# Attention on one core: a head's turned probabilities handed over by PSUM bank, three pieces of keys each

## The chip, the cores and the metric

The kernel runs on one core of one Trainium2 chip. The metric is the device time of one execution in microseconds (us): the median of several runs.

## The reference

A stack of two layers over 8 sequences of 100 tokens, width 512. Each layer is a gated cross-attention to a context of 722 rows and then a gated mixture of experts. The first attention is masked by padding, the second is not. What bears on the change is the attention, 16 heads of width 32:

```python
q = _split_heads(query @ w_q.T + b_q)
k = _split_heads(key_in @ w_k.T + b_k)
v = _split_heads(value @ w_v.T + b_v)
scores = jnp.einsum('bhqd,bhkd->bhqk', q, k) / jnp.sqrt(jnp.float32(D_K))
scores = jnp.where(mask == 0, jnp.float32(-1000000000.0), scores)
attn = jax.nn.softmax(scores, axis=-1)
out = jnp.einsum('bhqk,bhkd->bhqd', attn, v)
```

Here b is 8, h is 16, q is 100 and k is 722.

## The kernel before

The function `attention` is called once a layer. Its last block handles the 8 batches one after the other (`over_batches`), with every order written out by hand, engine by engine, and semaphores between them. Heads are taken in 4 groups of 4 (`NG`, `HPC`). Keys are cut in two ways: for scores and softmax into two segments of 362 and 360 (`SEG`), for the transposes and the weighted values into six pieces of 128, the last one of 82 (`KC`).

A batch is a run of "halves" h: one segment of one group of heads. In each half TensorE does these things in this order (`body`): the scores of the half (L427); in even halves the weighted values of an earlier group (`weighted_values`, L458); a piece of the next batch's keys or values (`make_piece`, L321 and L325); the transposes of one head of the half two before (`transposed`, L439), called the first or even head here; a second piece; and the transposes of the second or odd head. The halves 4 to 11 make one turn of the loop. The last of them has no pieces, and has the output projection (L468) between its two heads. In the last batch of a layer there is no next batch, so pieces are left out everywhere.

VectorE takes maxima of the scores (L537 masked, L541 unmasked), then factors and the normalising of the probabilities (L571), and the second part of each piece (L343, L349). ScalarE does the exponentials (L661), the first part of each key piece (L334), the heads' outputs (L652), parts of the next context (L353), and the copies of turned probabilities out of PSUM (`turned`, L647). In its order for a half come first the copy of the odd head of the half before, then two exponentials, a small operation, two exponentials, and at the end the copy of the even head.

The turned probabilities of one head are six pieces of 100 columns. They lie in the tile `pt`, 128 partitions by 2 banks of PSUM, three pieces in each bank. There is one such tile:

```python
pt = cx.enter_context(nc.psum_tensor(env.name("pt"), [P, 2, 512], F32))
```

TensorE writes all six pieces and counts up `t_mm` once. ScalarE copies both banks into `pTs` by one instruction and counts up `t_out` once. The transposes of the next head wait for that, and `weighted_values` waits for all four heads of its group. The exponentials wait on `t_mm`, since they overwrite `probs` of a head that has been turned.

Of the kernel before, what the change touches and what calls it, by code (L numbers as in the profile page):

```python
# [10 lines left out]
ACT = mybir.ActivationFunctionType  # L11
# [3 lines left out]
P = 128  # L15
B, S, D = 8, 100, 512
SK = 722
H, DH = 16, 32
DC = D // P
HPC = P // DH  # L20
# [3 lines left out]
KC = -(-SK // P)  # L24
# [94 lines left out]
def attention(nc, env, layer, masked, w_q, b_q, w_k, b_k, w_v, b_v, w_o, b_o):  # L119

    with ExitStack() as cx:
        def sb(n, s, dt=F32):
            return cx.enter_context(nc.sbuf_tensor(env.name(n), s, dt))

        def sem(n):
            return env.semaphore(n)

        x, xnT, ident = env.x, env.xnT, env.ident
# [103 lines left out]
        probs = [sb(f"probs{n}", [S, SK]) for n in range(2 * HPC)]  # L232
        pTs = sb("pTs", [P, 2, HPC, KC, S])
# [7 lines left out]
        pt = cx.enter_context(nc.psum_tensor(env.name("pt"), [P, 2, 512], F32))  # L241
# [13 lines left out]
        t_mm, t_out, pv_mm, ao_ready = sem("t_mm"), sem("t_out"), sem("pv_mm"), sem("ao_ready")  # L255
# [20 lines left out]
        def keys_of(kc):  # L276
            return P if kc < KC - 1 else KTAIL

        def at_half(b, p, h):

            return (b, p, h // 2, h % 2) if h < NHALF else (b + 1, 1 - p, h // 2 - NG, h % 2)
# [4 lines left out]
        def bank_of_heads(g):  # L286
            return (pp, po)[g % 2]
# [63 lines left out]
        def split_high(act, part):  # L351
            k0, k1 = SPLIT[part]
            act.activation(ctx[0][:, :, k0:k1], raw[:, :, k0:k1], ACT.Copy).then_inc(high_ready, 1)  # L353
# [7 lines left out]
        def over_batches(body):  # L361

            for b in range(B):
                body(b, b % 2, min(2, B - 1 - b))

        with nc.Block() as block:
# [49 lines left out]
            def _(pe):  # L416
# [14 lines left out]
                def transposed(b, g, j, very_first=False):  # L431
                    pe.wait_ge(norm_done, b * (2 * H) + (g * HPC + j) * 2 + 2)
                    if very_first:
                        pe.wait_ge(pt_clear, 1)
                    else:
                        pe.wait_ge(t_out, b * H + g * HPC + j)
                    for kc in range(KC):
                        n = keys_of(kc)
                        last = pe.transpose(pt[0:n, kc // 3, (kc % 3) * S:(kc % 3 + 1) * S],  # L439
                                            probs[g % 2 * HPC + j][:, kc * P:kc * P + n], ident[0:S, 0:S])  # L440
                    last.then_inc(t_mm, 1)

                def weighted_values(b, p, g, more):
                    pe.wait_ge(t_out, b * H + HPC * (g + 1))
                    pe.wait_ge(piece_out, b * NPIECE + NPIECE)
                    if g == 0:
                        pe.wait_ge(res_done, b + 1)
                    elif more:
                        read_out = {1: ("k", 1, 0), 2: ("v", 0), 3: ("v", 2)}[g]
                        pe.wait_ge(piece_out, b * NPIECE + (NPIECE + PIECES.index(read_out) + 1))  # L450
                    elif g >= 2:
                        pe.wait_ge(ao_ready, b * NG + (g - 1))
                    bank = bank_of_heads(g)
                    for kc in range(KC):
                        n = keys_of(kc)
                        for j in range(HPC):
                            h = g * HPC + j
                            last = pe.matmul(bank[j * DH:(j + 1) * DH, 0:S], v[p][0:n, kc, h * DH:(h + 1) * DH],  # L458
                                             pTs[0:n, g % 2, j, kc, :], start=kc == 0, stop=kc == KC - 1,
                                             skip_group_check=True)  # L460
                    last.then_inc(pv_mm, 1)
# [179 lines left out]
            @block.scalar  # L641
            def _(act):

                def turned(b, g, j):
                    act.wait_ge(pv_mm, b * NG + g + 1)
                    act.wait_ge(t_mm, b * H + g * HPC + j + 1)
                    act.activation(pTs[:, g % 2, j, :, :].rearrange("k (a c) q -> k a (c q)", a=2),  # L647
                                   pt[:, :, 0:3 * S], ACT.Copy).then_inc(t_out, 1)

                def heads_out(b, g):  # L650
                    act.wait_ge(pv_mm, b * NG + g + 3)
                    act.activation(aoT[:, g, :], bank_of_heads(g)[:, 0:S], ACT.Identity, bias=bv[:, g:g + 1])\  # L652
                        .then_inc(ao_ready, 1)

                def exponents(b, g, seg, heads, first=False):
                    k0, k1 = SEG[seg]
                    for j in heads:
                        if not first:
                            act.wait_ge(t_mm, b * H + (g * HPC + j - 7))
                        act.wait_ge(max_ready, b * (2 * H) + ((g * 2 + seg) * HPC + j + 1))  # L660
                        act.activation(probs[g % 2 * HPC + j][:, k0:k1], ps[j][0:S, 0:k1 - k0], ACT.Exp,  # L661
                                       bias=less_max[:, g, seg, j:j + 1], scale=-1.0 if masked else 1.0,
                                       accum_out=sums[:, g, seg, j:j + 1]).then_inc(exp_done, 1)

                def shares(b, g):
                    act.wait_ge(apart_done, b * NG + g + 1)
                    act.activation(share[:, g, :, :], apart[:, g, :, :], ACT.Exp).then_inc(share_done, 1)

                def next_high(b, part):
                    act.wait_ge(ctx_in, b * 16)  # L670
                    act.wait_ge(piece_mm, b * NPIECE + (PIECES.index(LAST_READER[part]) + 1 - NPIECE))
                    split_high(act, part)

                def first_piece(*what):
                    piece_high(act, what, 0)
                first_piece("k", 0, 0)
                first_piece("k", 0, 1)
                exponents(0, 0, 0, range(HPC), True)
                first_piece("k", 1, 0)
                first_piece("k", 1, 1)  # L680
                exponents(0, 0, 1, range(HPC), True)
                shares(0, 0)
                first_piece("k", 2, 0)
                first_piece("k", 2, 1)
                exponents(0, 1, 0, range(HPC), True)
                turned(0, 0, 0)
                turned(0, 0, 1)
                first_piece("k", 3, 0)
                exponents(0, 1, 1, range(HPC), True)
                shares(0, 1)  # L690
                first_piece("k", 3, 1)
                next_high(1, 0)
                turned(0, 0, 2)
                next_high(1, 1)
                next_high(1, 2)

                def body(b, p, left):
                    for h in HALVES:
                        bb, bp, g, seg = at_half(b, p, h)
                        tb, _, tg, late = at_half(b, p, h - 2)  # L700
                        lb, _, lg, l_late = at_half(b, p, h - 3)
                        pieces = BESIDE[h] if left else ()
                        if h < NHALF + 3 or left:
                            turned(lb, lg, 2 * l_late + 1)
                        active = h < NHALF or left
                        if active:
                            exponents(bb, g, seg, (0, 1))
                        if h % 2 == 0:
                            heads_out(b, h // 2 - 2)
                        elif pieces:  # L710
                            piece_high(act, pieces[0], b + 1)
                        if active:
                            exponents(bb, g, seg, (2, 3))
                            if seg == 1:
                                shares(bb, g)
                        if pieces and h % 2 == 0:
                            piece_high(act, pieces[0], b + 1)
                        if h < NHALF + 2 or left:
                            turned(tb, tg, 2 * late)
                        for what in pieces[1:]:  # L720
                            piece_high(act, what, b + 1)
                        if left == 2:
                            for part in {10: (0, 1), 11: (2,)}.get(h, ()):
                                next_high(b + 2, part)
                over_batches(body)
# [1164 lines left out]
```

## Time and profile before

| | us |
|---|---|
| median of 3 runs | 2391.73 |
| lowest and highest | 2384.24, 2392.93 |
| the profiled execution's own time | 2411.99 |
| its span | 2410.2 |
| TensorE busy (matmul) | 2152.3 |
| VectorE, ScalarE busy | 1293.2, 1007.2 |
| copies L647, 256 of them, busy | 172.5 |
| transposes L439, 1536 of them, busy | 182.7 |

The profile is of one execution. PE is TensorE's matmuls and PEld its weight loads, which run ahead of them. DVE is VectorE, ACT is ScalarE. In a row of the timeline the first number is the start in us, the second how long it took, the last (x6) how many alike instructions were merged; in brackets stands how long the engine was idle before, and what ended it. "Issue" is said where no semaphore event explains the end, and it can hide a wait that was over by the time of the next matmul.

### The profile page before, as it was taken

The numbers are of one execution on the slowest core, as the hardware profiler recorded it, in microseconds if no ns is written. First come the engines' busy times: TensorE is split into PE (matmuls) and PEld (weight loads), VectorE is DVE, ScalarE is ACT, GpSimd is POOL, SyncE is SP. The second block draws the span as 40 slices with busy tenths as digits, with TensorE's granted clock in tenths as the row PEclk, the third lists the DMA queues.
The fourth block names the chain that finished last, engine by engine and source line by source line (L and its number), as shares of the span: only waits on it lengthen the run. The fifth ranks groups of instructions, "written<-read, shape, count | busy, mean of one in ns | idle before, by whom it ended". The sixth has DMA issues, their size and how long they took to land. (4 is left out here: it accounts for less than half of the span.)

```text
span 2410.2 us, 39542 instructions
## 1 busy us (share of the span) xinstructions
PE 2152.3 (89%) x13422; PEld 1509.6 (63%) x13423; DVE 1293.2 (54%) x2824; ACT 1007.2 (42%) x2099; POOL 563.1 (23%) x556
## 2 busy tenths in 40 slices
PE   5999999977955999999939999999879988999995
PEld 3777777766922444444427777777669436777773
DVE  4677777765513222222256677777651106777776
ACT  2466666653200111111123666666533006566663
POOL 3000000002472455454521000000013202323321
PEclk9999999986987999999969999999969998999997
DMA  7000000003002999999641000000030006766642
GB/s 261 33 31 31 31 31 31 6 1 137 1 1 108 321 305 338 313 339 290 173 161 46 28 28 26 26 26 2 1 137 20 17 34 258 274 209 238 219 178 67
DMA packets 64819, 287.92 MB, mean 119 GB/s; under 512 B 11741, under 2 KB 12143, under 8 KB 45355
## 3 DMA queue, kind: packets, MB, share of 16 engines
q1 hardware_dynamic: 42842, 246.40, 27.2%
q0 software_dynamic: 21840, 39.69, 7.7%
q8 instruction: 87, 1.43, 0.2%
q14 instruction: 50, 0.40, 0.1%
HBM read 257.85 MB, written 33.96 MB: 121 GB/s over the span
## 5 line engine op out<-in xcount | busy, mean ns | idle before, releaser
L661 ACT ACTIVATE probs<-ps,less_max 100x362 f32<-100x362 f32 (+1 forms) x512 | 282.3, 563 | 145.2 <-DVE less_max L537 79.7
L1297 PE MATMUL pgu<-ring,xT 128*128 x560 | 267.4, 600 | 7.9 <-issue 4.3
L647 ACT ACTIVATE pTs<-pt 128x600 f32<-128x600 f32 x256 | 172.5, 674 | 160.4 <-PE pt L439 158.1
L439 PE MATMUL pt<-ident,probs 100*128 100x100 f32 (+1 forms) x1536 | 182.7, 256 | 43.9 <-ACT pTs L647 41.9
L439 PEld LDWEIGHTS pt<-ident,probs 100*128 100x128 f32 (+1 forms) x1536 | 153.2, 141 | 87.0 <-issue 59.5
L571 DVE TENSOR_SCALAR probs<-probs,factor 100x362 f32<-100x362 f32 (+1 forms) x512 | 178.1, 411 | 1.7
L1297 PEld LDWEIGHTS pgu<-ring,xT 128*128 128x128 f32 x560 | 99.7, 191 | 116.7 <-issue 116.5
L1343 ACT ACTIVATE sg<-pgu 128x256 f32<-128x256 f32 x70 | 26.8, 383 | 320.0 <-PE pgu L1297 320.0
L1654 DVE TENSOR_TENSOR ws_low<-w,ws_high 128x2048 fp32r<-128x2048 f32 x63 | 142.9, 2290 | 24.2 <-ACT ws_high L1585 24.2
L942 PE MATMUL pg<-wd,hT 128*100 128x512 f32 x256 | 115.1, 611 | 41.0 <-issue 37.1
L537 DVE CUSTOM_DVE_ANT_0 ps<-ps,madd 100x362 f32<-100x362 f32 (+1 forms) x256 | 128.7, 564 | 24.5 <-PE ps L427 24.3
L1373 DVE COPY hT<-ph 128x256 f32<-128x256 f32 x70 | 29.7, 424 | 197.6 <-PE ph L1303 197.6
L1311 PE MATMUL pd<-ring,hT 128*128 x280 | 132.9, 597 | 2.7 <-issue 1.8
L1585 ACT ACTIVATE ws_high<-w 128x2048 fp32r<-128x2048 f32 x63 | 120.6, 1918 | 24.8 <-PE pu L1534 20.6
L1249 POOL DMA_INDIRECT moe_sum<-y,sum_at x70 | 112.8, 1611 | 76.2 <-POOL sum_at L1244 51.5
L541 DVE TENSOR_REDUCE less_max<-ps 100x1 f32<-100x362 f32 (+1 forms) x256 | 118.4, 524 | 14.6 <-PE ps L427 13.5
L1365 DVE COPY xT<-px 128x512 f32<-128x512 f32 x71 | 49.1, 691 | 138.7 <-PE px L1279 138.7
L942 PEld LDWEIGHTS pg<-wd,hT 128*100 128x100 f32 x256 | 43.6, 172 | 111.4 <-issue 105.4
L1534 PE MATMUL pu<-ws_high,xT_high 128*128 128x512 f32 x240 | 108.2, 451 | 4.8 <-DVE ws_low L1654 4.8
L1339 ACT ACTIVATE y<-pd,slot_weight 128x512 f32<-128x512 f32 x70 | 48.1, 687 | 145.5 <-PE pd L1311 118.5
L1560 PE MATMUL pd<-w,hT 128*128 128x512 f32 x240 | 107.9, 592 | 0.0
L1477 POOL COPY index_now<-slot_token 128x1 uint32 (+1 forms) x16 | 31.2, 1947 | 318.6 <-PE px L1521 221.5
(261 smaller groups left out, 5070.2 us busy)
## 6 DMA issues: line engine op xcount, KB each, us to landing
ring<-in_l_ew SPq DMA_DIRECT2D x64, 1536.0 KB
w<-in_l_ew SPq DMA_DIRECT2D x64, 1024.0 KB, 8.2
xnT<-in_ctxT SPq DMA_DIRECT2D x14, 1444.0 KB, 6.6
wu<-in_l_up SPq DMA_DIRECT2D x2, 4096.0 KB, 12.7
b<-in_l_eb SPq DMA_DIRECT2D x8, 1024.0 KB, 4.6
moe_sum<-zrow SPq DMA_DIRECT2D x3, 2048.0 KB, 15.4
moe<-moe_sum SPq DMA_DIRECT2D x24, 200.0 KB
wd<-in_l_down SPq DMA_DIRECT2D x2, 2048.0 KB
```

The costliest lines, as they stand in the source:

```text
L439: last = pe.transpose(pt[0:n, kc // 3, (kc % 3) * S:(kc % 3 + 1) * S], probs[g % 2 * HPC + j][:, kc * P:kc * P + n], ident[0:S, 0:S])
L537: dve.tensor_tensor_reduce(out=scores, in0=scores, in1=madd[p][:, k0:k1], scale=-1.0, scalar=3.0e38, op0=ALU.add, op1=ALU.min, accum_out=l ...
L541: dve.tensor_reduce(least_of, scores, AX.X, ALU.max, negate=True).then_inc(max_ready, 1)
L571: dve.tensor_scalar(at, at, factor[:, g, seg, j:j + 1], None, ALU.mult).then_inc(norm_done, 1)
L647: act.activation(pTs[:, g % 2, j, :, :].rearrange("k (a c) q -> k a (c q)", a=2), pt[:, :, 0:3 * S], ACT.Copy).then_inc(t_out, 1)
L661: act.activation(probs[g % 2 * HPC + j][:, k0:k1], ps[j][0:S, 0:k1 - k0], ACT.Exp, bias=less_max[:, g, seg, j:j + 1], scale=-1.0 if masked ...
L942: last = pe.matmul(pg[n % 2][0:S, :], hT[:, hf * 8 + f, t * S:(t + 1) * S], wd[hf][:, f, :], start=f == 0, stop=f == 7)
L1249: pool.indirect_dma_start(out=env.moe_sum[p][:, :], in_=y[p][:, :], in_offset=None, compute_op=ALU.add, out_offset=bass.IndirectOffsetOnAx ...
L1297: last = pe.matmul(pgu[p][:, :], xT[p][:, c, :], wgu[c], start=c == 0, stop=c == DC - 1)
L1311: last = pe.matmul(pd[p][:, :], hT[p][:, f, :], wdn[f], start=f == 0, stop=f == FI - 1)
L1585: act.activation(ws[WS[q]][0][:, :, :], w[q][:, :, :], ACT.Copy).then_inc(w_high[q], 1)
L1654: dve.tensor_tensor(ws[WS[q]][1][:, :, :], w[q][:, :, :], ws[WS[q]][0][:, :, :].bitcast(F32), ALU.subtract).then_inc(w_low[q], 1)
```

## The change

The transposes of a head are handed over in two parts, one for each bank of `pt`. TensorE waits for the bank, writes three pieces, counts up `t_mm`, and does the same for the other bank. ScalarE copies each bank by an instruction of its own, 300 elements a partition in place of 600, and counts up `t_out` after each. All other waits on the two semaphores count twice as far, and so wait for the same as before.

```diff
-                    else:
-                        pe.wait_ge(t_out, b * H + g * HPC + j)
-                    for kc in range(KC):
-                        n = keys_of(kc)
-                        last = pe.transpose(pt[0:n, kc // 3, (kc % 3) * S:(kc % 3 + 1) * S],
-                                            probs[g % 2 * HPC + j][:, kc * P:kc * P + n], ident[0:S, 0:S])
-                    last.then_inc(t_mm, 1)
+                    for half in range(2):
+                        if not very_first:
+
+                            pe.wait_ge(t_out, 2 * (b * H + g * HPC + j) - 1 + half)
+                        for kc in range(3 * half, 3 * half + 3):
+                            n = keys_of(kc)
+                            last = pe.transpose(pt[0:n, half, (kc % 3) * S:(kc % 3 + 1) * S],
+                                                probs[g % 2 * HPC + j][:, kc * P:kc * P + n], ident[0:S, 0:S])
+                        last.then_inc(t_mm, 1)
...
-                    pe.wait_ge(t_out, b * H + HPC * (g + 1))
+                    pe.wait_ge(t_out, 2 * (b * H + HPC * (g + 1)))
...
-                    act.wait_ge(t_mm, b * H + g * HPC + j + 1)
-                    act.activation(pTs[:, g % 2, j, :, :].rearrange("k (a c) q -> k a (c q)", a=2),
-                                   pt[:, :, 0:3 * S], ACT.Copy).then_inc(t_out, 1)
+                    for half in range(2):
+                        act.wait_ge(t_mm, 2 * (b * H + g * HPC + j) + half + 1)
+                        act.activation(pTs[:, g % 2, j, 3 * half:3 * half + 3, :].rearrange("k c q -> k (c q)"),
+                                       pt[:, half, 0:3 * S], ACT.Copy).then_inc(t_out, 1)
...
-                            act.wait_ge(t_mm, b * H + (g * HPC + j - 7))
+                            act.wait_ge(t_mm, 2 * (b * H + (g * HPC + j - 7)))
```

## Rows read from the trace of the kernel before

**Rows 1.** Page, part 1: busy time, share of the span, instructions.
```profile
PE 2152.3 (89%) x13422; PEld 1509.6 (63%) x13423; DVE 1293.2 (54%) x2824; ACT 1007.2 (42%) x2099; POOL 563.1 (23%) x556
```

**Rows 2.** Windows, an inner and the last batch: length, busy by engine, granted clock, DMA.
```profile
334.00:391.00 57.00, 55.06 (x553) 44.85 (x552) 42.02 (x137) 36.78 (x99) 4.24 (x3) 1.00 0.10 33
506.00:563.00 57.00, 35.41 (x363) 23.30 (x361) 27.97 (x94) 23.63 (x63) 0.00 (x0) 0.72 0.08 26
```

**Rows 3.** Single lines' instructions: ns, lowest, median, highest; first and last start.
```profile
L97 ACT ACTIVATE xnT<-ln_pT x32: 503/504/506, 22.2 to 1784.0; 128x400 f32<-128x400 f32 x32
...
L647 ACT ACTIVATE pTs<-pt x256: 652/672/702, 80.0 to 1762.1; 128x600 f32<-128x600 f32 x128
...
L652 ACT ACTIVATE aoT<-pp,bv x32: 335/342/343, 105.9 to 1755.5; 128x100 f32<-128x100 f32 x32
...
L439 PE MATMUL pt<-ident,probs x1536: 247/249/429, 79.1 to 1761.7; 100*128 100x100 f32 x192
```

**Rows 4.** Timeline, ScalarE, a copy and the instruction behind it.
```profile
328.00 0.67 ACT L647 ACTIVATE pTs<-pt 128x600 f32<-128x600 f32 x1 [1.56 <-PE pt L439]
328.57 2.00 ACT L353 ACTIVATE ctx_high<-xnT 128x1024 fp32r<-128x1024 f32 x2
```

**Rows 5.** Timeline, ScalarE, unmasked layer: first exponential of an odd half.
```profile
1445.21 0.56 ACT L661 ACTIVATE probs<-ps,less_max 100x360 f32<-100x360 f32 x1 [0.57 <-DVE less_max L541]
```

**Rows 6.** Timeline, TensorE's weight loads: behind a key piece, and behind weighted values.
```profile
106.91 0.63 PEld L439 LDWEIGHTS pt<-ident,probs 100*128 100x128 f32 x6
...
324.33 0.19 PEld L325 LDWEIGHTS pp<-wv_high,ctx_high 128*128 128x128 f32 x1 [0.15 <-issue]
```

**Rows 7.** Timeline: the first head's copy and the second head's weight loads.
```profile
343.97 0.69 ACT L647 ACTIVATE pTs<-pt 128x600 f32<-128x600 f32 x1
...
344.78 0.52 PEld L439 LDWEIGHTS pt<-ident,probs 100*128 100x128 f32 x6 [0.23 <-issue]
...
350.86 0.52 PEld L439 LDWEIGHTS pt<-ident,probs 100*128 100x128 f32 x6 [0.27 <-issue]
...
1443.13 0.52 PEld L439 LDWEIGHTS pt<-ident,probs 100*128 100x128 f32 x6 [0.17 <-issue]
```

**Rows 8.** Timeline: weighted values behind scores, then a half without them.
```profile
365.70 0.68 PE L439 MATMUL pt<-ident,probs 100*128 100x100 f32 x6
366.31 0.42 PE L427 MATMUL ps<-kT_high,qb_high 32*100 32x362 f32 x4
366.48 0.67 ACT L647 ACTIVATE pTs<-pt 128x600 f32<-128x600 f32 x1 [2.65 <-PE pt L439]
367.20 1.02 PEld L458 LDWEIGHTS pp<-pTs,v 128*32 128x32 f32 x48 [0.47 <-ACT pTs L647]
...
373.59 0.41 PE L427 MATMUL ps<-kT_high,qb_high 32*100 32x360 f32 x4
...
374.27 0.19 PEld L325 LDWEIGHTS po<-wv_high,ctx_high 128*128 128x128 f32 x1 [0.26 <-issue]
```

**Rows 9.** Timeline at the turn of a batch.
```profile
336.54 0.68 ACT L647 ACTIVATE pTs<-pt 128x600 f32<-128x600 f32 x1
337.33 0.52 PEld L439 LDWEIGHTS pt<-ident,probs 100*128 100x128 f32 x6 [1.93 <-issue]
...
340.45 0.54 DVE L537 CUSTOM_DVE_ANT_0 ps<-ps,madd 100x362 f32<-100x362 f32 x1
```

**Rows 10.** Timeline in the last batches of both layers.
```profile
536.34 0.92 PEld L439 LDWEIGHTS pt<-ident,probs 100*128 100x128 f32 x6 [3.10 <-issue]
...
542.76 1.23 PE L439 MATMUL pt<-ident,probs 100*128 100x100 f32 x6 [0.91 <-ACT pTs L647]
544.09 0.67 ACT L647 ACTIVATE pTs<-pt 128x600 f32<-128x600 f32 x1 [1.48 <-PE pt L439]
544.87 0.92 PEld L439 LDWEIGHTS pt<-ident,probs 100*128 100x128 f32 x6 [1.23 <-issue]
...
1759.16 0.53 PEld L439 LDWEIGHTS pt<-ident,probs 100*128 100x128 f32 x6 [1.09 <-issue]
```

## The prediction

> **What bounds the kernel now.** I read the page first: TensorE is busy for 2152.3 of 2410.2 us [rows 1]. Whole-program shares say little of one stage, so the windows came next. In an inner batch of the masked attention (334 to 391 us) TensorE has work for 55.06 of 57.00 us at full clock, VectorE for 42.02 and ScalarE for 36.78; in the last batch of that layer, which has no next batch's keys and values to fill the gaps, TensorE is busy 35.41 of 57.00 us at a granted clock of 0.72 [rows 2]. So inner batches are bound by TensorE except for small pauses, and the last one by the chain from engine to engine. Then the timeline was walked through one batch, looking for idle time ahead of TensorE's weight loads (the PEld rows), and for who ended each. A turned head passes TensorE, PSUM, ScalarE's copy, and TensorE again, and pauses of four kinds hang on it.
>
> **Prices of the pieces.** The change replaces one copy of 600 elements by two of 300: 256 ScalarE instructions more. The copy of 400 takes 504 ns and that of 600 takes 672 ns, both plain copies out of PSUM [rows 3]. That is 0.84 ns an element over a constant of 168 ns, so I take 0.42 us for 300 (an estimate from these rows). The nearest smaller one, 100 elements with a bias, takes 342 ns, the bound from below; 504 ns is the bound from above. A ScalarE instruction that waits for nothing begins 0.10 us before the one before it ends (328.00 plus 0.67 against 328.57) [rows 4]. Two copies back to back then occupy 0.32 + 0.42 = 0.74 us in place of 0.67: 0.07 us more a head, 256 x 0.07 = 18 us of ScalarE in all. These lie in ScalarE's idle time: the exponentials after an odd head's copy wait 0.57 us for VectorE in the unmasked layer (the tighter of the two) [rows 5]. Without that cover the 18 us would count in full. The page "ScalarE: Activation LUTs" of the Trainium skill (What ACT_TABLE_LOAD costs) gives 186 ns plus 0.833 ns an element for such an instruction and 93 ns of overlap; by it the pair costs 0.093 us more than one, 24 us over the kernel, and would speak against the change wherever ScalarE were the bound. The rows above put it at 0.07.
>
> On TensorE the change adds 256 waits and 256 increments between pieces 3 and 4 of a head, no matmul. A wait that is already satisfied leaves no mark here: the six weight loads at 106.91 stand behind a key piece and two waits, and the row has no idle time ahead of it [rows 6]. I take 0 for a satisfied wait; the bound from above is the 0.15 us of idle weight loading left where the form of the tiles changes (324.33) [rows 6], that from below is 0, as a wait gives nothing back. In time, six transposes take 0.68 us of which the last is 0.25 [rows 3, 8], so they follow each other by 0.086 us and the third is done 0.26 us before the sixth. DMAs, VectorE and GpSimd issue what they did.
>
> **Where it pays, inner batches.** *The second head of a half.* Its transposes wait for the first head's copy. Copy at 343.97 for 0.69, weight loads at 344.78 after 0.23 idle; at the next half 350.86 after 0.27; unmasked 1443.13 after 0.17 [rows 7]. With two banks the first three transposes need only the copy that ends at +0.42, 0.25 us earlier, and the next three follow behind the second copy (ends at +0.74; they come up at +0.42 + 0.12 + 0.26 = 0.80). So the pause goes. The masked layer has 13 such places (6 batches with both halves, one with one): 13 x 0.25 = 3.2 us. In the unmasked one I count 7 x 0.25 and 6 x 0.12, as there VectorE gives the next maxima little earlier: 2.5 us. They count in full, since copy, transposes, scores and maxima of the next half are one chain there.
>
> *The weighted values.* The odd head's transposes start at 365.70, its copy at 366.48, and the weighted values at 367.20, 0.89 us after the scores began; where no copy is waited for the next product comes 0.68 us after the scores (373.59 to 374.27) [rows 8]. So 0.21 us is lost. Counted from the first transpose t: before, the copy ends at t + 1.45. After, piece 3 ends at t + 0.42, first copy t + 0.52 to t + 0.94, second from t + 0.84 to t + 1.26. Gain 0.19. Such pauses stand at three of the four groups of a batch, 3 x 7 x 2 = 42: 8.0 us. The fourth lies beside VectorE's chain and brings nothing.
>
> *The turn of the batch.* The longest pause, 1.93 us before 337.33, ends with a copy that began at 336.54 [rows 9]. It would end 0.25 us sooner, but the chain that decides runs beside it, from the exponentials through the factors and the normalising on VectorE to the maxima at 340.45, ahead of which VectorE has no idle time [rows 9], and these set the next exponentials; I count 0 of it. What is late next there is VectorE, by as much as before. The masked layer's first weighted values may even come 0.07 us later, as ScalarE is full there; two layers, 0.1 us.
>
> **Where it pays, the last batches.** Four second heads a layer stand in the open chain (one of them 536.34, after 3.10 us idle) [rows 10], each 0.25 us sooner, and the weighted values behind the last of them another 0.25: 1.25 a layer. Then come four heads with nothing between them. At half clock one cycle is transposes at 542.76, copy at 544.09, next weight loads at 544.87, so 2.14 us; four of them 8.5 us [rows 10]. With two banks: third transpose done at 0.34 + 0.38 = 0.72, copy 0.82 to 1.24, the bank written again at 1.39; the other bank follows 0.51 behind. Three cycles of 1.39 and a last of 1.80 make 6.0: 2.5 us. In the unmasked layer part of it runs at full clock (1.09 us idle before 1759.16 for 1.23) [rows 10], by the same steps 7.5 to 5.5: 2.0 us. Sum of both layers 2 x 1.25 + 4.5 = 7.0 us. With copies of 0.342 us, the lower bound, little is added: the pauses of inner batches are used up (42 x 0.21), the last batches give some 1.5 more, together 23.
>
> **Sum.** 3.2 + 2.5 + 8.0 + 7.0 - 0.1 = 20.6 us, with the profiled execution's own 2412.0 us becoming 2391.4 (span 2410.2 to 2389.6). That execution was 20 us slower than the median, 0.8%; the pauses are waits of fixed length, so I take the same 20.6 off 2391.7: 2371 us.
>
> **Rivals.**
> *A, no overlap of the two copies* (a wait for TensorE stands between them). The pair ends at 0.84: second heads gain 0.11, weighted values 0.09. 24 x 0.11 + 42 x 0.09 + 10 x 0.10 + 4.3 = 11.7 us, so 2380. For it: no row shows such a pair. Against it: the waits ahead of other ScalarE instructions don't stop the early start.
> *B, small copies are dear* (0.504 us, the upper bound, and no overlap). Weighted values lose 0.08, second heads 0.06, the last four heads of a layer still gain about 2: -3.4 - 1.6 - 0.7 + 3.9 = about -2, so 2394, no change. The slope between 400 and 600 elements speaks against it.
> *C, TensorE pauses between the pieces* (the other side). If the wait in the middle of a head stops the weight loads from running ahead, each of 256 heads pays in a stream that TensorE bounds. The nearest row is the 0.15 us left by a change of form [rows 6]; 256 x 0.15 = 38 us against a gain of 21: 2409. It breaks even at 0.08 us a head and is slower by 0.5% from 0.13. Against it stands the row at 106.91, and that a matmul in front of a wait is in flight while the next one is fetched.
> *D, the clock holds longer.* If the shorter idle times keep the last batches at full clock, their matmuls shorten (1.23 us a head against 0.68). A clock of 0.72 over 57 us means half speed in some 32 us of them [rows 2]; at a busy share of 0.62 that is 20 us of matmuls, 10 too many, of which I take 6 to stand in the chain, and 4 in the other layer: 2361. Against it, the 3.10 us pause before 536.34 only shrinks to 2.85 [rows 10].
> *E, nothing happens,* because the copy was never what was waited for: the second row of each pair in [rows 7, 8] follows the copy's end by 0.05 to 0.12 us every time, so I count this within B.
>
> **How the numbers follow.** Forecast 0.64, A 0.13, B 0.07, C 0.06, D 0.10. The measurement tells about 0.5% (12 us) from no change. D, nearly all of the forecast and half of A are beyond it: faster 0.77. Half of A, B and the forecast's lower edge: same 0.17. C: slower 0.06. Range: D's 2361 less 3 of spread, and up past A's 2380 to 2386, which leaves out B and C, 0.13, and the odd end of D.
>
> **What would show it.** Two copies of about 0.42 us per head with 0.32 between their starts; no idle ahead of second heads in inner batches; weighted values at about 0.70 after the scores; copies beginning about 0.26 us before the sixth transpose is done; four final heads 1.4 us apart. A gap inside a head's six weight loads in inner batches would mean C; copies of 0.5 us B; starts 0.42 apart A. A gain below 12 us with all pauses gone would mean that they were cover for something that I took for idle.

## The result, and the profile after

The changed kernel takes 2367.2 us (median of 6 runs, 2360.4 to 2374.2) against 2388.5 us (median of 6 runs) of the kernel before: ratio 0.9915, 95% interval 0.989 to 0.9939, or 21 us less (15 to 26). The forecast was 20.6 us less, at 2371 us. Two later series of the same kernel, told below, gave 0.9933 and 0.9929, or 16 and 17 us.

The page of the changed kernel, busy time by engine and the two groups of instructions that changed (line, busy us, mean ns, idle time before, and what ended it):

```profile
PE 2142.5 (91%) x13422; PEld 1513.5 (64%) x13423; DVE 1292.4 (55%) x2824; ACT 1013.9 (43%) x2355; POOL 566.0 (24%) x556
...
L650 ACT ACTIVATE pTs<-pt 128x300 f32<-128x300 f32 x512 | 189.4, 425 | 124.7 <-PE pt L441 123.5
L441 PE MATMUL pt<-ident,probs 100*128 100x100 f32 (+1 forms) x1536 | 185.3, 259 | 33.6 <-ACT pTs L650 31.6
```

The single line's instructions, ns lowest, median, highest:

```profile
L650 ACT ACTIVATE pTs<-pt x512: 402/421/460, 80.3 to 1714.4; 128x300 f32<-128x300 f32 x171
```

ScalarE has 256 instructions more. Its copies are busy for 189.4 us in place of 172.5, 17 more for 18 forecast; its busy time as a whole grew by only 7 us, and what became of the rest was not followed. Each copy takes 421 ns, where 420 had been worked out [rows 3].

The timeline of an inner batch. First the second heads and the weighted values behind them, to be laid beside [rows 7, 8]:

```profile
341.91 0.76 ACT L650 ACTIVATE pTs<-pt 128x300 f32<-128x300 f32 x2
342.47 0.62 PEld L441 LDWEIGHTS pt<-ident,probs 100*128 100x128 f32 x6
342.63 0.68 PE L441 MATMUL pt<-ident,probs 100*128 100x100 f32 x6
343.24 0.41 PE L427 MATMUL ps<-kT_high,qb_high 32*100 32x360 f32 x4
343.29 0.72 ACT L650 ACTIVATE pTs<-pt 128x300 f32<-128x300 f32 x2
...
347.86 0.73 ACT L650 ACTIVATE pTs<-pt 128x300 f32<-128x300 f32 x2
348.40 0.61 PEld L441 LDWEIGHTS pt<-ident,probs 100*128 100x128 f32 x6
348.74 0.56 ACT L334 ACTIVATE kT_high<-pp,bk 128x360 fp32r<-128x360 f32 x1 [0.15 <-PE pp L321]
349.15 0.41 PE L427 MATMUL ps<-kT_high,qb_high 32*100 32x362 f32 x4
349.20 0.72 ACT L650 ACTIVATE pTs<-pt 128x300 f32<-128x300 f32 x2
349.98 1.02 PEld L460 LDWEIGHTS po<-pTs,v 128*32 128x32 f32 x48 [0.41 <-ACT pTs L650]
...
378.21 0.68 PE L441 MATMUL pt<-ident,probs 100*128 100x100 f32 x6
378.73 0.73 ACT L650 ACTIVATE pTs<-pt 128x300 f32<-128x300 f32 x2 [2.62 <-PE pt L441]
378.82 0.41 PE L427 MATMUL ps<-kT_high,qb_high 32*100 32x362 f32 x4
379.51 1.02 PEld L460 LDWEIGHTS po<-pTs,v 128*32 128x32 f32 x48 [0.27 <-ACT pTs L650]
```

Neither second head (342.47 and 348.40) has idle time ahead of its weight loads any more, and there is no gap inside the six. The two copies of a head together take 0.72 to 0.76 us, and where ScalarE is free a pair begins 0.52 us after the head's first transpose (378.21 to 378.73), with the sixth still under way; it was 0.78 us [rows 8]. At 379.51 the weighted values start 0.69 us after the scores (0.89 before). At 349.98 it is 0.83 us: there the copies had to wait for a key piece (348.74) on ScalarE.

The turn of the batch:

```profile
334.48 0.74 ACT L650 ACTIVATE pTs<-pt 128x300 f32<-128x300 f32 x2
335.02 0.52 PEld L441 LDWEIGHTS pt<-ident,probs 100*128 100x128 f32 x6 [1.96 <-issue]
...
338.39 0.54 DVE L539 CUSTOM_DVE_ANT_0 ps<-ps,madd 100x362 f32<-100x362 f32 x1
```

The second head starts 0.54 us after the first head's copies began, where it was 0.79 [rows 9], and the maxima come 3.91 us after that same start of the copies, as before. The pause is as long as it was; nothing is won here.

The four heads at the end of the masked layer:

```profile
537.18 0.92 PEld L441 LDWEIGHTS pt<-ident,probs 100*128 100x128 f32 x6 [0.48 <-issue]
538.58 0.92 PEld L441 LDWEIGHTS pt<-ident,probs 100*128 100x128 f32 x6 [0.48 <-issue]
```

One follows the other by 1.40 us, where 1.39 was forecast and 2.14 was before [rows 10].

For lengths of batches I take the starts of the residual on VectorE (`x<-pp,gate,x`), which comes once a batch. Of the kernel before, one inner and the last batch of the masked layer, and between them the second head of [rows 7] with the scores behind it:

```profile
219.96 0.75 DVE L612 SCALAR_TENSOR_TENSOR x<-pp,gate,x 100x512 f32<-100x512 f32 x1
278.75 0.75 DVE L612 SCALAR_TENSOR_TENSOR x<-pp,gate,x 100x512 f32<-100x512 f32 x1
...
344.81 0.71 PE L439 MATMUL pt<-ident,probs 100*128 100x100 f32 x6
345.45 0.41 PE L427 MATMUL ps<-kT_high,qb_high 32*100 32x360 f32 x4
...
512.82 0.75 DVE L612 SCALAR_TENSOR_TENSOR x<-pp,gate,x 100x512 f32<-100x512 f32 x1 [0.34 <-PE pp L468]
557.10 0.75 DVE L612 SCALAR_TENSOR_TENSOR x<-pp,gate,x 100x512 f32<-100x512 f32 x1 [17.89 <-PE pp L468]
```

and of the changed kernel:

```profile
219.28 0.75 DVE L614 SCALAR_TENSOR_TENSOR x<-pp,gate,x 100x512 f32<-100x512 f32 x1
277.38 0.75 DVE L614 SCALAR_TENSOR_TENSOR x<-pp,gate,x 100x512 f32<-100x512 f32 x1
...
508.85 0.75 DVE L614 SCALAR_TENSOR_TENSOR x<-pp,gate,x 100x512 f32<-100x512 f32 x1
548.65 0.75 DVE L614 SCALAR_TENSOR_TENSOR x<-pp,gate,x 100x512 f32<-100x512 f32 x1 [13.67 <-PE pp L470]
```

An inner batch goes from 58.79 to 58.10 us and the last one from 44.28 to 39.80. In the same manner, for every profile of this case (us; inner is the usual batch; attention is from the first residual of a layer to its eighth, summed over both layers, so each layer's first batch is left out of it; experts is from the eighth residual of the masked layer to the first of the other, and holds the first batch of the unmasked layer):

```
kernel                    inner, masked / not   last, masked / not   attention   experts
before                        58.8 / 58.7         44.3 / 41.7          788.5      820.2
before, again                 58.9 / 58.7         46.0 / 41.5          790.7      814.3
changed                       58.1 / 58.0         39.8 / 41.8          775.7      787.1
changed, second time          58.1 / 58.0         41.0 / 41.0          776.1      790.1
changed, third time           58.1 / 58.0         39.8 / 39.7          773.4      794.0
copies only                   59.2 / 59.0         47.3 / 45.4          800.2      793.6
TensorE only                  58.9 / 58.7         46.1 / 44.8          794.4      789.4
last batches only             58.9 / 58.7         40.5 / 39.5          782.9      798.5
early reading only            58.4 / 58.3         43.7 / 41.4          784.1      822.2
early release only            58.8 / 58.6         43.3 / 43.8          789.1      810.5
key piece behind              58.0 / 57.9         40.4 / 38.5          771.4      790.4
with GpSimd's part            56.6 / 56.6         39.8 / 40.8          760.6      811.2
```

The attention has become 14.6 us shorter (mean of two profiles against mean of three). The two profiles first compared differ by 46.5 us of span, 33 of them in the experts. That is not the change's: the experts took 810 to 822 us in all four profiles of one series (before at 2414.8 us), whichever kernel, and 787 to 799 in those of the three others (before at 2386 to 2388.5 us), with kernels that don't gain among them. The three later series ran on three chips, so chip and series can't be told apart. The first profile of before, an execution of 2412.0 us with 820.2 us of experts, resembles the slower series.

### The profile page after: what moved, and what is told of

Read it like the earlier page. It is cut to its first block and busy times, and to the rows that moved or that the text cites. A ratio compares the mean times of both kernels' runs of the same rounds, so it can differ in the third digit from the quotient of the medians.

```text
span 2363.7 us, 39798 instructions
## 1 busy us (share of the span) xinstructions
PE 2142.5 (91%) x13422; PEld 1513.5 (64%) x13423; DVE 1292.4 (55%) x2824; ACT 1013.9 (43%) x2355; POOL 566.0 (24%) x556
## 5 line engine op out<-in xcount | busy, mean ns | idle before, releaser
L650 ACT ACTIVATE pTs<-pt 128x300 f32<-128x300 f32 x512 | 189.4, 425 | 124.7 <-PE pt L441 123.5
L945 PE MATMUL pg<-wd,hT 128*100 128x512 f32 x256 | 110.3, 593 | 2.3 <-issue 1.6
L664 ACT ACTIVATION_READ_ACCUMULATOR probs<-ps,less_max 100x1 f32 x512 | 104.5, 204 | 0.0
```

The source lines that it names most:

```text
L650: act.activation(pTs[:, g % 2, j, 3 * half:3 * half + 3, :].rearrange("k c q -> k (c q)"), pt[:, half, 0:3 * S], ACT.Copy).then_inc(t_out, 1)
L945: last = pe.matmul(pg[n % 2][0:S, :], hT[:, hf * 8 + f, t * S:(t + 1) * S], wd[hf][:, f, :], start=f == 0, stop=f == 7)
```

## The experiments

Each edit is shown against the changed kernel.

**The changed kernel once more.** No edit.

> The changed kernel once more, with more rounds and a profile of its own. Three theories of where its 21 us came from. Theory 1 (handover alone): the time is won in the attention and nowhere else; there the two profiles differ by about 13 us, so the ratio to the kernel before would be about 0.9945, and the 33 us by which the first layer's experts were shorter in its profile are spread between executions: this profile's expert stage (from the last residual of the first attention to the first one of the second) may lie anywhere between 780 and 825 us. Theory 2 (experts gain too): the earlier end of the attention shortens the experts in every execution; the ratio stays near 0.991 and the stage stays near 787 us. Attention in this profile within 1 us of the first one's 387.5 and 388.2 by either, unless TensorE's clock in the last batches differs.

2369.2 us against 2386.1, ratio 0.9933, interval 0.9916 to 0.995, between the two theories' figures. The experts took 790.1 us, which either theory allows; the attention was within 1 us of the first profile in sum. What decides is the same series' next two kernels: they gain nothing in the attention, and their experts took 793.6 and 789.4 us. So the 33 us are not the handover's, and theory 1 is left.

**The copies alone.**

```diff
-                        if not very_first:
-                            pe.wait_ge(t_out, 2 * (b * H + g * HPC + j) - 1 + half)
+                        if half == 0 and not very_first:
+                            pe.wait_ge(t_out, 2 * (b * H + g * HPC + j))
...
-                        last.then_inc(t_mm, 1)
+                    last.then_inc(t_mm, 2)
```

> Only ScalarE's copy is cut in two; TensorE still writes all six pieces, signals once, and waits for both copies. If the pair costs 0.07 us more than one copy: second heads of the two halves behind the turn start 0.07 us later, weighted values 0.06 later, 42 + 26 places, about 3 to 5 us slower than before the change (ratio 1.001 to 1.002). The rival, dear copies of 0.5 us without overlap, gives 0.33 us a place, over 20 us slower. The rival that the copies alone bring the gain gives a ratio below 1.

2393.6 us, ratio 1.0033 (1.0022 to 1.0044): 8 us slower, more than the 3 to 5 expected. The inner batch is 0.3 us longer. That is 0.07 us at each of its five places; what I had left out of the sum are the last batches, 47.3 and 45.4 us. The copies alone bring nothing, and a loss of 8 us in place of over 20 puts rival B, 0.5 us for each copy, out.

**TensorE's side alone.**

```diff
-                    for half in range(2):
-                        act.wait_ge(t_mm, 2 * (b * H + g * HPC + j) + half + 1)
-                        act.activation(pTs[:, g % 2, j, 3 * half:3 * half + 3, :].rearrange("k c q -> k (c q)"),
-                                       pt[:, half, 0:3 * S], ACT.Copy).then_inc(t_out, 1)
+                    act.wait_ge(t_mm, 2 * (b * H + g * HPC + j) + 2)
+                    act.activation(pTs[:, g % 2, j, :, :].rearrange("k (a c) q -> k a (c q)", a=2),
+                                   pt[:, :, 0:3 * S], ACT.Copy).then_inc(t_out, 2)
```

> Only TensorE's side is cut in two: it waits ahead of each bank and signals behind each, but ScalarE waits for both signals and copies both banks by one instruction that frees both. If the waits and signals in the middle of a head are free, the attention takes what it took before the change, inner batches 58.8 and 58.7 us, ratio 1.000. If they make TensorE pause, as the rival in the prediction had it, 256 heads at 0.08 to 0.15 us give 20 to 38 us more, and the changed kernel would have gained that much more without them.

2387.5 us, ratio 1.001 (0.9999 to 1.002). Its batch in the masked layer:

```profile
220.88 0.75 DVE L613 SCALAR_TENSOR_TENSOR x<-pp,gate,x 100x512 f32<-100x512 f32 x1
279.77 0.75 DVE L613 SCALAR_TENSOR_TENSOR x<-pp,gate,x 100x512 f32<-100x512 f32 x1
```

58.89 us, at most 0.1 us more than before for the 16 heads of a batch, so some 5 ns for a wait and a signal in the middle of a head. The upper end of the ratio, 1.002, would allow 19 ns (4.8 us for 256 heads). Rival C had 80 to 150 ns.

**The last batches alone.**

```diff
+                    split = b == B - 1
...
-                            pe.wait_ge(t_out, 2 * (b * H + g * HPC + j) - 1 + half)
+                            if split:
+                                pe.wait_ge(t_out, 2 * (b * H + g * HPC + j) - 1 + half)
+                            elif half == 0:
+                                pe.wait_ge(t_out, 2 * (b * H + g * HPC + j))
...
-                        last.then_inc(t_mm, 1)
+                        if split:
+                            last.then_inc(t_mm, 1)
+                    if not split:
+                        last.then_inc(t_mm, 2)
...
+                    if not (b == B - 1):
+                        act.wait_ge(t_mm, 2 * (b * H + g * HPC + j) + 2)
+                        act.activation(pTs[:, g % 2, j, :, :].rearrange("k (a c) q -> k a (c q)", a=2),
+                                       pt[:, :, 0:3 * S], ACT.Copy).then_inc(t_out, 2)
+                        return
```

> The whole change, but only in the last batch of each layer; the other batches hand over a whole head with one copy. Theory 1: inner batches 58.8 and 58.7 us as before; last batch of the masked layer about 40 us from residual to residual in place of 44.3, that of the unmasked layer 41.7 in place of 41.7 or down to 38 if the clock stays at full speed; in sum 4.5 us faster, ratio 0.998. Theory 2 (the experts gain from an earlier end of the attention): the stage between the attentions is also near 787 us and the ratio near 0.994 or less.

2382.0 us, ratio 0.9976 (0.9962 to 0.999): 5.7 us faster (2 to 9). That is what the last batches are worth, as timed over the whole program. In its profile they took 40.5 and 39.5 us, the inner ones 58.9 and 58.7 as before, the experts 798.5: the earlier end of the attention did not shorten them.

**The kernel before, again.** No edit to it.

> The kernel before once more, for a second profile. If the first profile's 820 us of experts were spread between executions, this one has 787 to 800 us there, and the time is near 2386. If the last batches (44.3 and 41.7 us in the first profile, against 46.1 and 44.8 us in the kernel with only TensorE's side cut) depend on when TensorE's clock falls, they come out between 44 and 47 us here; inner batches 58.8 and 58.7 us again.

2408.7 us (one execution), and 2414.8 us by the median of 21 more: this series is slower for all kernels. The experts took 814.3 us, as in the first profile of before and not as expected: they go with the series. Last batches 46.0 and 41.5 us, the second of them below the 44 to 47 expected; the masked one varies by 1.8 us between two executions of one kernel.

**Early reading alone.** ScalarE is signalled after each bank; TensorE waits for both copies.

```diff
-                        if not very_first:
-                            pe.wait_ge(t_out, 2 * (b * H + g * HPC + j) - 1 + half)
+                        if half == 0 and not very_first:
+                            pe.wait_ge(t_out, 2 * (b * H + g * HPC + j))
```

> One half of the handover alone: ScalarE starts copying a bank as soon as its three pieces are there, but TensorE gets the tile back only when both banks are copied. Weighted values should gain as in the whole change (0.19 us by the prediction's steps, where ScalarE is free), second heads should start about 0.07 us later than before the change, as the pair ends 0.07 us later. By that the inner batch lies near 58.4 us (58.8 before, 58.1 with the whole change); last batches gain a fourth to a half of the whole change. Ratio 0.996 to 0.998. The rival, that both gains come from the bank being given back, puts it at 1.000 or above.

Ratio 0.997 (0.9957 to 0.9984). Inner batch 58.4 us, as expected. A second head and the weighted values behind it:

```profile
291.90 0.52 PEld L440 LDWEIGHTS pt<-ident,probs 100*128 100x128 f32 x6 [0.30 <-issue]
293.26 1.02 PEld L459 LDWEIGHTS po<-pTs,v 128*32 128x32 f32 x48 [0.28 <-ACT pTs L649]
```

The head waits a little longer than before the change (0.30 us against 0.23 and 0.27), and the weighted values stand where no copy holds them.

**Early release alone.** ScalarE is signalled once for six pieces; each copy gives its bank back.

```diff
-                        last.then_inc(t_mm, 1)
+                    last.then_inc(t_mm, 2)
```

> The other half alone: TensorE signals once after six pieces, two copies follow, and each gives its bank back. Second heads start as early as in the whole change; weighted values come 0.06 us later than before the change. The profile of the changed kernel shows that the second heads gained 0.12 to 0.15 us each and not 0.25, as a pause of the weight loads is not wholly a pause of the matmuls. So inner batches near 58.8 us, no gain; last batches shorter than before by less than in the whole change. Ratio 0.998 to 1.001. The prediction's own step (0.25 us for each second head) would give 58.5 us.

Ratio 0.9988 (0.9965 to 1.0011); inner batch 58.8 us.

```profile
292.49 0.61 PEld L440 LDWEIGHTS pt<-ident,probs 100*128 100x128 f32 x6
294.20 1.02 PEld L459 LDWEIGHTS po<-pTs,v 128*32 128x32 f32 x48 [0.53 <-ACT pTs L649]
```

The mirror image: no idle time ahead of the head, 0.53 us ahead of the weighted values (0.47 before). The prediction's step of 0.25 us for each second head would have given 58.5 us here, so that step was too large; this is told below.

By attention time, early reading gives 5.5 of the 14.6 us, early release 0.5, and both together 8.6 more than the two. Some 4 us of that surplus are in inner batches (one of early reading's took 1.4 us longer than the others) and some 4 in the last ones. There the cycle of the four final heads shows it, first with early reading alone, then with early release alone:

```profile
542.83 0.92 PEld L440 LDWEIGHTS pt<-ident,probs 100*128 100x128 f32 x6 [0.92 <-issue]
544.66 0.92 PEld L440 LDWEIGHTS pt<-ident,probs 100*128 100x128 f32 x6 [0.92 <-issue]
```
```profile
543.96 0.92 PEld L440 LDWEIGHTS pt<-ident,probs 100*128 100x128 f32 x6 [0.98 <-issue]
545.86 0.92 PEld L440 LDWEIGHTS pt<-ident,probs 100*128 100x128 f32 x6 [0.98 <-issue]
```

In stretches with a granted clock of 0.50 a cycle is 2.14 us before the change [rows 10], 1.83 and 1.90 with one half of it, and 1.40 with both: 0.31 and 0.24 us won apart, 0.74 together.

**The change, and two of VectorE's instructions to GpSimd.** Abridged; waits on `low_ready` are split between it and `low_pool`, and two loops written out.

```diff
+                    for part in range(2):
+                        k0, k1 = SPLIT[part]
+                        pool.wait_ge(high_ready, b * NS + part + 1)
+                        pool.sem_inc(passed, 1)
+                        pool.tensor_tensor(ctx[1][:, :, k0:k1], raw[:, :, k0:k1],
+                                           ctx[0][:, :, k0:k1].bitcast(F32), ALU.subtract).then_inc(low_pool, 1)
...
-                            for part in {10: (0, 1), 11: (2,)}.get(h, ()):
+                            for part in {11: (2,)}.get(h, ()):
```

> The whole change, and the low parts of the next context's first two pieces (1024 elements each, L358, 2.35 us of VectorE a batch) are computed by GpSimd in place of VectorE. It tests the statement that the pause of 1.9 us at the turn of a batch is VectorE's doing: if so the maxima of half 11 start 1.7 us sooner behind the scores, the pause falls from 1.96 us to near 0.2, and six inner batches of each layer take 56.3 to 57.3 us in place of 58.1 and 58.0, 10 to 20 us in all (ratio to the kernel before 0.985 to 0.989). GpSimd takes 1.05 us for 400 elements, so some 2.7 us for each part, beside idle time. Rivals: the pause belongs to the copy of the turned head, then nothing changes there; or GpSimd and VectorE slow each other (VectorE's instructions beside it longer than in the other profiles), then less is gained.

2376.9 us against 2414.8, ratio 0.9849 (0.9826 to 0.9872), with an inner batch of 56.6 us:

```profile
158.54 0.75 DVE L624 SCALAR_TENSOR_TENSOR x<-pp,gate,x 100x512 f32<-100x512 f32 x1
...
215.18 0.75 DVE L624 SCALAR_TENSOR_TENSOR x<-pp,gate,x 100x512 f32<-100x512 f32 x1
...
322.33 4.34 POOL L422 TENSOR_TENSOR ctx_low<-xnT,ctx_high 128x1024 fp32r<-128x1024 f32 x2 [18.05 <-ACT ctx_high L359]
...
324.81 0.54 DVE L549 CUSTOM_DVE_ANT_0 ps<-ps,madd 100x360 f32<-100x360 f32 x1 [0.67 <-PE ps L437]
...
327.76 0.74 ACT L660 ACTIVATE pTs<-pt 128x300 f32<-128x300 f32 x2
328.30 0.71 PEld L451 LDWEIGHTS pt<-ident,probs 100*128 100x128 f32 x6 [0.45 <-issue]
```

The maxima of half 11 now wait for the scores and not for VectorE, and the idle time ahead of the turn's second head falls from 1.96 to 0.45 us, of which 0.26 stand between any two loads of the output projection. So that pause was VectorE's, as the prediction had it; what writing out the two loops did was not tried apart. This kernel beats both: 1.5% below before, 0.8% below the change alone by the ratios of two series.

**A key piece moved behind the copies.**

```diff
                             turned(lb, lg, 2 * l_late + 1)
+                        if h == 6 and left:
+                            piece_high(act, BESIDE[5][1], b + 1)
...
-                        for what in pieces[1:]:
+                        for what in (pieces[1:] if h != 5 else ()):
                             piece_high(act, what, b + 1)
```

> The changed kernel with one ScalarE instruction moved: in half 5 the first part of the second key piece (L334) is done behind the copies of the odd head in place of ahead of them. It tests why the weighted values of half 6 gained only 0.07 us where the other two gained 0.2: if that instruction holds the first copy up, the idle time before them falls from 0.41 to 0.27 us and an inner batch from 58.1 to 57.97 us. If the 0.13 us have another cause (VectorE's next maxima, the tile of the pieces), the idle time stays at 0.4. The delayed piece may make VectorE's maxima 0.13 us later, which should cost nothing there.

One execution, 2363.5 us, read for its trace. The inner batch is 57.98 us in place of 58.11, and the idle time is that of the other groups:

```profile
346.74 0.73 ACT L650 ACTIVATE pTs<-pt 128x300 f32<-128x300 f32 x2 [0.48 <-PE pt L441]
347.36 0.57 ACT L334 ACTIVATE kT_high<-pp,bk 128x360 fp32r<-128x360 f32 x1
347.53 1.02 PEld L460 LDWEIGHTS po<-pTs,v 128*32 128x32 f32 x48 [0.28 <-ACT pTs L650]
```

**The changed kernel a third time.** No edit.

> The changed kernel a third time. The attention is shorter by some 14 to 15 us in the profiles; two series gave ratios of 0.9915 and 0.9933. If the attention is all, this one should give 0.994 (0.9925 to 0.9955). If something outside it gains 5 us more in every execution, it gives 0.991 to 0.992 again.

2371.9 us against 2388.4, ratio 0.9929 (0.9913 to 0.9945): inside what was given for the attention alone, near its lower end. The interval reaches into the other range (0.991 to 0.992) too, so this run does not decide. The attention was 773.4 us.

## Why the prediction was right, point by point

*The prices.* A copy of 300 elements takes 421 ns, the pair 0.72 to 0.76 us with 0.30 us between the two starts (median; 0.32 forecast), the wait in the middle of a head some 5 ns. All three terms held; rivals A, B and C are out. (A's sum counts 24 second heads and the forecast's 26, which makes 0.2 us.) By the Trainium skill's page "ScalarE: Activation LUTs" (What ACT_TABLE_LOAD costs) the pair would take 0.093 us more than one copy, an estimate from its 186 ns a copy less 93 ns of overlap; the trace has 0.05 to 0.07.

*The weighted values.* Where ScalarE is free, 0.89 became 0.69 us: 0.20 for a forecast of 0.19. In one group of three it was 0.07, as a key piece stood ahead of the copies; moving it brought the missing 0.13 us. The step failed in taking ScalarE to be free at all three places. 14 batches of 0.47 us make 6.5 us, for 8.0.

*The second heads.* Mis-sized: 0.25 us each was forecast. Matmul by matmul, in inner batches before and after, the two second heads of a masked batch gained 0.12 and 0.13 us, those of an unmasked one 0.08 and 0.14. The rows show a reason: the weight loads' idle time is not the matmuls'. Undisturbed, the loads run 0.16 us ahead of their matmuls (342.47 to 342.63); after a wait it is 0.03 (344.78 [rows 7] to 344.81). So 0.13 us of each pause cost nothing. That makes some 0.24 us a batch, 3.3 us in all, for 5.7. Early release alone gained the same 0.12 and 0.13 there.

*What stands beside VectorE's chain.* The same comparison shows one gain that the prediction does not list, 0.31 us at the head ahead of the output projection, and three losses: 0.17 at the key piece that waits for the heads' outputs (0.10 in the unmasked layer), 0.04 at the turn and 0.10 at the weighted values of the fourth group, whose idle time grew from 0.47 to 0.57 us. They cancel, but for 0.05 us in the unmasked layer. So an inner batch is shorter by what the other five places gave, 0.7 us.

*The turn of the batch* brought 0, as forecast, and GpSimd's experiment showed why.

*The last batches.* The cycle of the four last heads was right, 1.40 for 1.39 us. The sum was 7.0 us forecast. In the masked layer the batch fell by 3.3 to 6.2 us (44.3 and 46.0 to 39.8, 41.0, 39.8; 3.8 forecast), in the other by -0.3 to 2.0 (41.7 and 41.5 to 41.8, 41.0, 39.7; 3.3 forecast). What is missing there is clock. The windows of that unmasked batch before and after (length, busy by engine, granted clock, DMA):

```profile
1728.00:1770.00 42.00, 27.09 (x327) 18.83 (x325) 18.01 (x54) 18.92 (x51) 0.00 (x0) 0.72 0.01 1
```
```profile
1682.00:1724.00 42.00, 32.03 (x327) 21.64 (x325) 17.86 (x53) 20.41 (x64) 0.00 (x0) 0.59 0.01 1
```

The same 327 matmuls are busy 5 us longer. So the pauses won were paid back in this execution by a clock of 0.59 in place of 0.72, the reverse of rival D. At a like clock the term holds: the kernel with TensorE's side alone, which in all its inner batches is like the kernel before, had 0.62 in this batch and took 44.8 us, and the changed kernel 41.8 us at 0.59, 3.0 us less for 3.3 forecast. In the masked layer it went rival D's way: the clock of the last batch was 0.65 and 0.59 in the two profiles before and 0.70 to 0.71 in the three after, and its matmuls were busy 28.8 and 31.8 us before, 28.3 to 28.9 after. So up to 3 us of the gain there are clock. Why the clock falls at one time and not at another, with the same instructions, was not found. Timed, the kernel with the last batches alone changed gained 5.7 us, for 7.0.

*The sum.* By the profiles the inner batches gave 8.9 us and the last ones 5.7, together 14.6. The first batch of each layer, which that count leaves out, gave about 1 us more: from its first scores to the first residual, 96.9 us became 96.3 in the unmasked layer, 99.7 and 99.6 became 99.3, 99.4 and 98.3 in the masked one. So some 15.6 us are seen, for 20.6 forecast. The timed runs say 21, 16 and 17 (intervals 15 to 26, 12 to 20, 13 to 21); 15.6 lies within all three, so they ask for no gain outside the attention and do not rule out a small one. That the first series met the forecast to 1 us is luck: the mechanism was right, but the terms were too large, their sum by about a third, and one of the three groups of weighted values was not free as the prediction took it to be.

## What to carry to other kernels

Handing a tile over by bank needs both halves of the handshake: the early signal moved what reads the data, the early release what writes the tile, and either alone gave two fifths of the gain or next to nothing (ratios 0.997 and 0.9988, against 0.9915 to 0.9933). When a pause is priced, take the time from start to start of what follows, not the idle time of the weight loads, and look for what stands in the copying engine's queue at the new, earlier time. The largest pause beside a handover can be another engine's work; here moving that was worth as much again.

## What the runs showed that I had not expected

In the masked layer, the fourth batch after the first residual took 58.38 us in place of 58.11, in all three profiles of the changed kernel. There the copies of one head begin 0.28 us late (0.80 us after the first transpose):

```profile
363.29 0.68 PE L441 MATMUL pt<-ident,probs 100*128 100x100 f32 x6
364.09 0.73 ACT L650 ACTIVATE pTs<-pt 128x300 f32<-128x300 f32 x2 [2.87 <-PE pt L441]
364.87 1.02 PEld L460 LDWEIGHTS pp<-pTs,v 128*32 128x32 f32 x48 [0.55 <-ACT pTs L650]
```

It is the place from which the prediction had read its own row (366.48 and 367.20 [rows 8]), and in this batch nothing was gained there: the idle time was 0.47 us before. This batch is 0.24 to 0.29 us longer than its neighbours in every profile whose inner batches have two copies a head, copies only and early release only among them, and not in those with one (before 58.81, TensorE only 58.90). So it comes with the second copy; nothing in the trace names the cause.

And GpSimd did its two subtractions of 1024 elements in 4.34 us without slowing the VectorE instructions that ran beside it, all of which read PSUM: the maxima took 564 ns in the mean, beside GpSimd and elsewhere, and the value pieces 687 against 691.
